# Causal attention inside a two-layer block: two score sets of the last batch in other buffers, two groups of weighted sums a set, and twenty unread products instead of twelve

## The chip, the cores and the metric

The kernel runs on one core of one Trainium2 chip. The metric is device time in microseconds (us) from one launch to its end; less is better. The engines are named as the profile names them: PE (TensorE, the matrix products), PEld (its weight loads), DVE (VectorE), ACT (ScalarE), POOL (GpSimd) and SP (SyncE, which here issues nearly all DMAs; SPq is its DMA queue).

## The reference, cut to what matters

The input x is 4 batches of 512 tokens of width 128. Two layers follow each other, each with feed-forward parts and an attention; the change touches only the softmax attention of the first layer, with 16 heads of width 8:

```python
qk = x @ w_attn.T + b_attn
q, k, v = (_heads(q), _heads(k), _heads(x))
scores = jnp.einsum('bhqd,bhkd->bhqk', q, k) * scale
scores = jnp.where(causal, scores, -jnp.inf)
y_ar = jnp.einsum('bhqk,bhkd->bhqd', jax.nn.softmax(scores, axis=-1), v)
```

A second, linear attention over the same heads uses the error `e = v[1:] - y_ar[:-1]`, so it can't start before `y_ar` of the batch is there. After the attention come a feed-forward part, eight routed experts, a recurrent linear attention and the experts once more.

## The kernel before, in words

**Sizes.** A batch has 512 tokens, cut into NT = 4 tiles of 128. The 16 heads are taken in NS = 4 sets of HL = 4 heads; one product on PE covers a tile of keys (or queries) times a tile of the other side for the four heads of a set, 512 columns. Causality leaves 10 tile pairs a set. A pair on the diagonal takes a second product, which adds the mask.

**Two passes.** The softmax needs the row maximum before the exponentials. Pass one ("maxima", `max_scores`, L1541) forms the scores with the queries as rows, pair by pair, alternately in two PSUM banks (`max_banks`, L134, one of `ps_turn`, one of `ps_accum`), and DVE reduces each (`maxima`, L1100, recorded on L1104). Maximum product m waits until reduction m-2 is done. Pass two ("scores", L1561) forms them again with the keys as rows, two pairs to a *unit*, alternately in the two halves of `ps_pair`; there the row maximum rides along as one more row of the operand, so that ACT can take the exponential of a whole unit at once (L846, recorded as `sb_work<-ps_pair`). Unit u waits until exponential u-2 is done. A batch has 20 units, five to a set (i = 0 to 4).

**Weighted sums.** `answers(b, hs, kt)` (L1576) multiplies the exponentials of key tile kt with the values. The four heads go to four groups of 32 columns of the array (shape 128*32 in the profile, where all other products here are 128*128). Key tile 0 has 512 columns, tile 1 has 384, tiles 2 and 3 have 256 and 128. After the fourth, ACT copies the set's sums out (`answers_out`, L832, recorded on L837). In ACT's order this copy stands behind the first exponential of the next set, and the second one stands behind the copy.

**Order of the work on PE** (`attention`, L1626). At step u PE issues the scores of unit u+2, one maximum product of the *next* batch, the weighted sums that are due, and a second maximum product. The sums due at step i of a set are, by L1643, key tile 0 at i = 1, tile 1 at i = 3, tiles 2 and 3 at i = 4; at i = 1 the previous set's sums are also transposed (`turn_answers`, L1588). The last batch (b = 3) has no next batch, so its steps hold no maxima. Within a batch the maxima of a set are called m0 to m9 below, two to a step: m6 and m7 at i = 3, m8 and m9 at i = 4. DVE also does work of the previous batch among the first set's maxima (a layer norm: L1001 to L1010).

**Order of the DMAs on SP** (a list written out by hand; `hold` at L310 is a wait on a semaphore). `load_exp_set` (L352) brings a set for pass two: four issues into `ring` slot 0 or 1 (L356) and one of keys into `x_sets` (L358); `max_row` (L396) then lays the row maxima into that slot. `load_max_set` (L360) does the same for pass one into `ring` slots 2 and 3 and `m_sets`. Each set has two slots that the sets take in turn, so set hs+2 can be loaded only when set hs has been read. In the loop over batches SP loads the state of the linear attention (`load_state`, L375) and the next values (`load_values`, L382), and then for each set `next_max_set(b + 1, hs)` (L388: waits for the ten maxima of that set and refills their slot) and the refill of the score slot. For the last two sets of the last batch `next_max_set` waits and loads nothing.

**Before the attention** PE runs `stay_awake(12, ...)` (L1717; L1439): products whose result nothing reads, recorded as `ps_pair<-sb_ident_bf,sb_ones_bf`. They stand ahead of batch 0's first scores, which wait for a set with its row of maxima.

Of the kernel before, what the change touches and what calls it, by code (L numbers as in the profile page):

```python
# [27 lines left out]
F32 = mybir.dt.float32  # L28
# [7 lines left out]
P = 128  # L36
D = 128
B, T = 4, 512
NT = T // P
# [64 lines left out]

MAX_PAIRS = [(qt, kt) for qt in range(NT) for kt in range(qt + 1)]
EXP_PAIRS = [(kt, qt) for kt in range(NT) for qt in range(kt, NT)]
DIAGONAL = [EXP_PAIRS.index((t, t)) for t in range(NT)]
LAST_OF_UNIT = [EXP_PAIRS[2 * i + 1][0] for i in range(NPAIR // 2)]
NM, NX, NG_X = NS * NPAIR, NS * NPAIR // 2, NPAIR // 2
STEPS = NS * NT  # L110
# [2 lines left out]
def build(nc, x_in, bias_cols, w_attn_t, w_k2_t, w_proj_t, b_proj, w1_t, w2_t, b2,  # L113
          l1_w, l1_bv, l1_wp, l1_bp, wr, mw1, mw2, consts, out):
    ctx = ExitStack()
    with ctx:
# [193 lines left out]
        def hold(eng, sem, value):  # L310


            eng.wait_ge(sem, value)
            eng.sem_inc(s["held"], 1)
# [5 lines left out]
        def _(sp):  # L320
# [61 lines left out]
            def load_values(b):  # L382
# [2 lines left out]
                    hold(sp, s["v_aug"], b)  # L385
                sp.dma_start(values_of[b % 2][:], v_scr[b].rearrange("(t p) d -> p t d", p=P)).then_inc(s["v_in"], 16)

            def next_max_set(b, hs):  # L388

                hold(sp, s["smax_mm"], NM * b + NPAIR * (hs + 1))  # L390
                if hs + 2 < NS:
                    load_max_set(b, hs + 2)
                elif b + 1 < B:
                    load_max_set(b + 1, hs + 2 - NS)

            def max_row(b, hs):  # L396

                sp.dma_start(ring[3 * HD:3 * HD + 1, hs % 2].bitcast(F32),
                             mT[HL * hs:HL * hs + HL].bitcast(F32)).then_inc(s[f"xset{hs % 2}"], 16)

            def keep_values(b):

# [53 lines left out]
            for b in range(B):  # L456
                load_state(b)
                if b + 1 < B:
                    load_values(b + 1)
                for hs in range(NS):  # L460
                    if b + 1 < B:
                        next_max_set(b + 1, hs)
                    hold(sp, s["st_mm"], NX * b + NG_X * (hs + 1))
                    if hs + 2 < NS:
                        load_exp_set(b, hs + 2)
                        max_row(b, hs + 2)
                    elif b + 1 < B:
                        load_exp_set(b + 1, hs + 2 - NS)
                if b + 1 < B:
                    hold(sp, s["max_t_evac"], b + 2)  # L470
                    for hs in range(2):
                        max_row(b + 1, hs)
            for scr in xe_scr:
                spill = scr[0:NTOK].rearrange("(p r) d -> p r d", p=P)
# [951 lines left out]
        def _(pe):  # L1426
            def mm(dst, lhsT, rhs, start=True, stop=True):
                return pe.matmul(dst, lhsT, rhs, start=start, stop=stop, skip_group_check=True)  # L1428
# [132 lines left out]
            def scores(b, u):  # L1561

                hs, i = u // NG_X, u % NG_X
                if i == 0:
                    pe.wait_ge(s[f"xset{hs % 2}"], 96 * (2 * b + hs // 2 + 1))
                if u >= 2:
                    pe.wait_ge(s["exp_done"], NX * b + u - 1)
                for a in range(2):
                    kt, qt = EXP_PAIRS[2 * i + a]
                    last = mm(pair[u % 2][:, a, :], tile(x_sets[:, hs % 2], kt), ring[:, hs % 2, :, qt * P:(qt + 1) * P],  # L1570
                              stop=kt != qt)
                    if kt == qt:
                        last = mm(pair[u % 2][:, a, :], ident_bf[:], bc(add_k_bf[:], HL), start=False)
                last.then_inc(s["st_mm"], 1)
# [51 lines left out]
            def attention(b):  # L1626
# [9 lines left out]
                for u in range(NX):  # L1636
# [3 lines left out]
                    if ahead:  # L1640
                        max_scores(b + 1, 2 * u, 2 * u + 1)
                    for kt in range(NT):
                        if (DIAGONAL[kt] + NT - kt - 1) // 2 == i:  # L1643
                            answers(b, hs, kt)
                    if hs and i == 1:
                        turn_answers(b, hs - 1)
# [67 lines left out]
            pe.wait_ge(s["ma_k"], B)  # L1714
            pe.wait_ge(s["ffn_x"], B)
            pe.wait_ge(s["ka_tok"], B)
            stay_awake(12, pair[1][:, 1])  # L1717
            pe.wait_ge(s["max_t_evac"], 1)
            for b in range(B):
                attention(b)  # L1720
# [289 lines left out]
```

## Time and profile before

| what | value |
|---|---|
| time of the kernel, median of 3 runs | 661.89 us (658.84 to 665.67) |
| span of the profiled execution | 656.1 us |
| PE, DVE, ACT, POOL busy in that span | 82%, 55%, 30%, 29% |
| mean granted clock of PE, as a share of full speed | 0.946 |
| softmax and linear attention, four batches | 114.8 to 346.5 us of the span |

The profiled execution has a span, from its first to its last instruction; its own device time isn't listed apart from that. The median of the runs is 5.8 us above the span. Times in the rows are us from the start of the span. A matrix product's recorded length includes its way through the pipeline, so products overlap: what one costs is the distance from its start to the start of the next.

### The profile page before, as it was taken

The numbers are of one execution on the slowest core, as the hardware profiler recorded it, in microseconds if no ns is written. First come the engines' busy times: TensorE is split into PE (matmuls) and PEld (weight loads), VectorE is DVE, ScalarE is ACT, GpSimd is POOL, SyncE is SP. The second block draws the span as 40 slices with busy tenths as digits, with TensorE's granted clock in tenths as the row PEclk, the third lists the DMA queues.
The fourth block names the chain that finished last, engine by engine and source line by source line (L and its number), as shares of the span: only waits on it lengthen the run. The fifth ranks groups of instructions, "written<-read, shape, count | busy, mean of one in ns | idle before, by whom it ended". The sixth has DMA issues, their size and how long they took to land.

```text
span 656.1 us, 10406 instructions
## 1 busy us (share of the span) xinstructions
PE 537.0 (82%) x3895; PEld 330.7 (50%) x3895; DVE 359.9 (55%) x942; ACT 197.1 (30%) x282; POOL 189.0 (29%) x228
## 2 busy tenths in 40 slices
PE   1878676999899898988887987994887878888893
PEld 0655332444544453454355763882455555554593
DVE  5653666466676856683063562222686978833121
ACT  1354231543144334515613630211321311110120
POOL 6575562011020102011111167462310311322153
PEclk9996789799999999999998997996998999968998
DMA  7217878732352353215199823222575274100220
GB/s 269 115 38 242 277 230 265 174 108 66 96 154 58 114 110 92 72 45 138 49 144 148 256 90 109 78 70 76 161 201 152 62 200 127 50 33 27 89 72 10
DMA packets 73666, 79.85 MB, mean 122 GB/s; under 512 B 10946, under 2 KB 50499, under 8 KB 73360
## 3 DMA queue, kind: packets, MB, share of 16 engines
q1 hardware_dynamic: 71056, 73.61, 40.9%
q0 software_dynamic: 2560, 5.58, 2.5%
q8 instruction: 31, 0.51, 0.3%
q14 instruction: 19, 0.16, 0.1%
HBM read 44.07 MB, written 35.72 MB: 122 GB/s over the span
## 4 chain that ended last, share of the span: by engine, by line
PE 51%; DVE 18%; issue 7%; DMA 7%; SPq 5%; ACT 5%; POOL 5%; POOLq 0%; DVEq 0%; ACTq 0%
PE ps_accum L1428 23%; PE ps_pair L1428 18%; PE ps_turn L1428 6%; DMA sb_ring<-sb_qs 3%; PE ps_turn L1436 3%; SPq L356 2%; DVE sb_work L1178 2%; POOL sb_rstd L569 2%; DVE sb_stats L1001 2%; DVE sb_mpart L1104 1%; SPq L350 1%; DVE sb_work L1323 1%; POOL xe_scr L589 1%; DMA sb_expert_rows<-xe_scr 1%; DVE sb_mv L1004 1%
## 5 line engine op out<-in xcount | busy, mean ns | idle before, releaser
L846 ACT ACTIVATE sb_work<-ps_pair 128x1024 f32<-128x1024 f32 x80 | 80.3, 1026 | 55.8 <-PE ps_pair L1428 54.9
L1104 DVE TENSOR_REDUCE sb_mpart<-ps_turn 128x4 f32<-128x512 f32 x80 | 55.0, 688 | 32.4 <-PE ps_turn L1428 32.3
L1428 PE MATMUL ps_pair<-sb_ring,sb_xsets 128*128 128x512 f32 x160 | 64.5, 480 | 9.7 <-DMA sb_ring<-sb_qs 5.5
L1104 DVE TENSOR_REDUCE sb_mpart<-ps_accum 128x4 f32<-128x512 f32 x80 | 55.1, 688 | 19.3 <-PE ps_accum L1428 18.6
L1428 PE MATMUL ps_pair<-sb_ident_bf,sb_ones_bf 128*128 128x512 bf16 x189 | 51.0, 426 | 12.3 <-DMA sb_x<-y_scr 8.0
L1428 PE MATMUL ps_accum<-sb_work,sb_v_aug 128*32 128x128 f32 (+3 forms) x768 | 58.2, 397 | 0.3 <-ACT sb_work L846 0.3
L1428 PE MATMUL ps_turn<-sb_ring,sb_m_sets 128*128 128x512 f32 x80 | 39.0, 487 | 9.3 <-DVE sb_mpart L1104 9.0
L1428 PE MATMUL ps_accum<-sb_ring,sb_m_sets 128*128 128x512 f32 x80 | 41.4, 518 | 4.3 <-DVE sb_mpart L1104 3.8
L567 POOL TENSOR_SCALAR sb_ve<-sb_mv 128x4 f32<-128x4 f32 x24 | 5.5, 228 | 136.3 <-DVE sb_mv L1004 131.1
L650 POOL TENSOR_TENSOR sb_e_pad<-sb_v_next,sb_y_ar 128x128 f32<-128x128 f32 x16 | 7.3, 459 | 126.5 <-DVE sb_y_ar L1148 126.5
L1428 PEld LDWEIGHTS ps_pair<-sb_ring,sb_xsets 128*128 128x128 f32 x160 | 30.7, 199 | 20.8 <-issue 7.8
L1323 DVE TENSOR_TENSOR sb_work<-ps_pair,sb_cst 128x1024 f32<-128x1024 f32 x32 | 37.5, 1215 | 1.3 <-PE ps_pair L1428 1.2
L1178 DVE TENSOR_TENSOR sb_work<-ps_pair,sb_cst 128x1024 f32<-128x1024 f32 x32 | 37.7, 1219 | 0.9
L1428 PEld LDWEIGHTS ps_pair<-sb_ident_bf,sb_ones_bf 128*128 128x128 bf16 x189 | 19.8, 108 | 36.4 <-issue 10.9
L1428 PE MATMUL ps_accum<-sb_mw,sb_work 128*128 128x128 f32 x256 | 31.3, 276 | 2.7 <-issue 2.7
L589 POOL DMA_INDIRECT xe_scr<-sb_exit_rows,sb_slot_all x16 | 15.9, 995 | 59.5 <-DVE sb_slot_all L1085 55.9
L1272 DVE SCALAR_TENSOR_TENSOR sb_y_tmp<-ps_accum,sb_expert_rows 128x128 f32<-128x128 f32 x32 | 9.8, 347 | 42.0 <-PE ps_accum L1428 42.0
L1428 PE MATMUL ps_pair<-sb_y_tmp,sb_mw 128*128 128x256 f32 x128 | 30.7, 383 | 2.0 <-ACT sb_y_tmp L902 2.0
L1428 PE MATMUL ps_pair<-sb_xs,sb_w1r 128*128 128x512 f32 x64 | 23.5, 498 | 10.1 <-DVE sb_xs L1020 6.9
L1428 PEld LDWEIGHTS ps_accum<-sb_mw,sb_work 128*128 128x128 f32 x256 | 30.0, 192 | 3.1 <-issue 3.0
L1428 PEld LDWEIGHTS ps_accum<-sb_ring,sb_m_sets 128*128 128x128 f32 x80 | 15.4, 192 | 25.6 <-DVE sb_mpart L1104 18.5
L1428 PEld LDWEIGHTS ps_accum<-sb_work,sb_v_aug 128*32 128x32 f32 x768 | 17.4, 110 | 21.3 <-issue 13.0
(251 smaller groups left out, 1013.6 us busy)
## 6 DMA issues: line engine op xcount, KB each, us to landing
sb_expert_rows<-xe_scr SPq DMA_DIRECT2D x16, 258.0 KB, 2.7
sb_m_sets<-q_scr SPq DMA_DIRECT2D x16, 256.0 KB
sb_xsets<-k_scr SPq DMA_DIRECT2D x16, 256.0 KB
sb_ka_stk<-mk_scr SPq DMA_DIRECT2D x4, 1024.0 KB
xe_scr<-sb_cst SPq DMA_DIRECT2D x4, 1024.0 KB, 13.6
sb_mw<-in_mw SPq DMA_DIRECT2D x16, 256.0 KB, 5.8
sb_ka_stk<-mk_scr SPq DMA_DIRECT2D x8, 512.0 KB
q_scr<-sb_qs SPq DMA_DIRECT2D x12, 256.0 KB, 3.4
```

Source lines behind the costliest of these rows:

```text
L356: sp.dma_start(ring[VW * hl:VW * hl + 3 * HD, i, hl].bitcast(F32), head_rows(q_scr, b, HL * hs + hl, 3 * HD)).then_inc(done, 16)
L569: pool.tensor_tensor(rstd[i][:], ve[i][:], const("minus_half"), ALU.pow).then_inc(s["rstd"], 1)
L589: pool.indirect_dma_start(xe_scr[m], bass.IndirectOffsetOnAxis(ap=slot_all[:, i:i + 1], axis=0), rows_out[m][b][:, t, :], None).then_inc(s ...
L650: pool.tensor_tensor(dst, value, answer, ALU.subtract).then_inc(s["err_pad"], 1)
L846: act.activation(banks[:, 2 * i:2 * i + 2], pair[u % 2][:], ACT.Exp, scale=SCALE).then_inc(s["exp_done"], 1)
L1001: dve.bn_stats(stats[i][:, t, :], src[:, t, :]).then_inc(s["stats"], 1)
L1104: dve.tensor_reduce(mpart[:, m // NPAIR, m % NPAIR, :], max_banks[m % 2][:].rearrange("p (h k) -> p h k", h=HL), AX.X, ALU.max).then_inc(s ...
L1178: dve.tensor_tensor(work[:, n % 4].rearrange("p a (h q) -> p (a h) q", h=HL), pair[n % 2][:].rearrange("p a (h q) -> p (a h) q", h=HL), bc ...
L1272: last = dve.scalar_tensor_tensor(out=ye[n % 2][:, g, :], in0=accum[n % 2][:, g * D:(g + 1) * D], scalar=xg[:, n % 4, g, GATE:GATE + 1], i ...
L1323: dve.tensor_tensor(work[:, n % 4].rearrange("p a (h q) -> p (a h) q", h=HL), pair[n % 2][:].rearrange("p a (h q) -> p (a h) q", h=HL), bc ...
L1428: return pe.matmul(dst, lhsT, rhs, start=start, stop=stop, skip_group_check=True)
L1436: last = pe.transpose(tile(dst, t), src[:, t, 0:D], ident)
```

## The change

It does three things.

1. Sets 2 and 3 of the last batch are loaded into the `ring` slots 2 and 3 and into `m_sets`, the buffers of the maxima, once the last maxima have read them (`load_late_set`, called by `next_max_set`). All four rows of maxima of the last batch are laid in one after another, behind `max_t_evac`. The loads that the last batch issued between its own sets are gone, and `scores` takes these two sets from the other slots.
2. The sums of key tile 1 move from step i = 3 to step i = 4, where they stand directly ahead of those of tiles 2 and 3 (`ANSWERS_BEHIND`). This holds in all four batches.
3. `stay_awake` ahead of the attention runs 20 products instead of 12.

```diff
--- before.py
+++ after.py
@@ -104,7 +104,7 @@
 
 MAX_PAIRS = [(qt, kt) for qt in range(NT) for kt in range(qt + 1)]
 EXP_PAIRS = [(kt, qt) for kt in range(NT) for qt in range(kt, NT)]
-DIAGONAL = [EXP_PAIRS.index((t, t)) for t in range(NT)]
+ANSWERS_BEHIND = [1, 4, 4, 4]
 LAST_OF_UNIT = [EXP_PAIRS[2 * i + 1][0] for i in range(NPAIR // 2)]
 NM, NX, NG_X = NS * NPAIR, NS * NPAIR // 2, NPAIR // 2
 STEPS = NS * NT
@@ -385,6 +385,14 @@
                     hold(sp, s["v_aug"], b)
                 sp.dma_start(values_of[b % 2][:], v_scr[b].rearrange("(t p) d -> p t d", p=P)).then_inc(s["v_in"], 16)
 
+            def load_late_set(hs):
+
+                i, done = hs - 2, s[f"mset{hs - 2}"]
+                for hl in range(HL):
+                    sp.dma_start(ring[VW * hl:VW * hl + 3 * HD, hs, hl].bitcast(F32),
+                                 head_rows(q_scr, B - 1, HL * hs + hl, 3 * HD)).then_inc(done, 16)
+                sp.dma_start(m_sets[:, i].bitcast(F32), set_rows(k_scr, B - 1, hs)).then_inc(done, 16)
+
             def next_max_set(b, hs):
 
                 hold(sp, s["smax_mm"], NM * b + NPAIR * (hs + 1))
@@ -392,11 +400,14 @@
                     load_max_set(b, hs + 2)
                 elif b + 1 < B:
                     load_max_set(b + 1, hs + 2 - NS)
+                else:
+                    load_late_set(hs)
 
             def max_row(b, hs):
 
-                sp.dma_start(ring[3 * HD:3 * HD + 1, hs % 2].bitcast(F32),
-                             mT[HL * hs:HL * hs + HL].bitcast(F32)).then_inc(s[f"xset{hs % 2}"], 16)
+                late = b == B - 1 and hs >= 2
+                sp.dma_start(ring[3 * HD:3 * HD + 1, hs if late else hs % 2].bitcast(F32),
+                             mT[HL * hs:HL * hs + HL].bitcast(F32)).then_inc(s[f"mset{hs - 2}" if late else f"xset{hs % 2}"], 16)
 
             def keep_values(b):
 
@@ -461,14 +472,16 @@
                     if b + 1 < B:
                         next_max_set(b + 1, hs)
                     hold(sp, s["st_mm"], NX * b + NG_X * (hs + 1))
+                    if b == B - 1:
+                        continue
                     if hs + 2 < NS:
                         load_exp_set(b, hs + 2)
                         max_row(b, hs + 2)
-                    elif b + 1 < B:
+                    else:
                         load_exp_set(b + 1, hs + 2 - NS)
                 if b + 1 < B:
                     hold(sp, s["max_t_evac"], b + 2)
-                    for hs in range(2):
+                    for hs in range(NS if b + 2 == B else 2):
                         max_row(b + 1, hs)
             for scr in xe_scr:
                 spill = scr[0:NTOK].rearrange("(p r) d -> p r d", p=P)
@@ -1561,13 +1574,17 @@
             def scores(b, u):
 
                 hs, i = u // NG_X, u % NG_X
-                if i == 0:
+                late = b == B - 1 and hs >= 2
+                slot, keys = (hs, m_sets[:, hs - 2]) if late else (hs % 2, x_sets[:, hs % 2])
+                if i == 0 and late:
+                    pe.wait_ge(s[f"mset{hs - 2}"], 80 * 2 * B + 96)
+                elif i == 0:
                     pe.wait_ge(s[f"xset{hs % 2}"], 96 * (2 * b + hs // 2 + 1))
                 if u >= 2:
                     pe.wait_ge(s["exp_done"], NX * b + u - 1)
                 for a in range(2):
                     kt, qt = EXP_PAIRS[2 * i + a]
-                    last = mm(pair[u % 2][:, a, :], tile(x_sets[:, hs % 2], kt), ring[:, hs % 2, :, qt * P:(qt + 1) * P],
+                    last = mm(pair[u % 2][:, a, :], tile(keys, kt), ring[:, slot, :, qt * P:(qt + 1) * P],
                               stop=kt != qt)
                     if kt == qt:
                         last = mm(pair[u % 2][:, a, :], ident_bf[:], bc(add_k_bf[:], HL), start=False)
@@ -1640,7 +1657,7 @@
                     if ahead:
                         max_scores(b + 1, 2 * u, 2 * u + 1)
                     for kt in range(NT):
-                        if (DIAGONAL[kt] + NT - kt - 1) // 2 == i:
+                        if ANSWERS_BEHIND[kt] == i:
                             answers(b, hs, kt)
                     if hs and i == 1:
                         turn_answers(b, hs - 1)
@@ -1714,7 +1731,7 @@
             pe.wait_ge(s["ma_k"], B)
             pe.wait_ge(s["ffn_x"], B)
             pe.wait_ge(s["ka_tok"], B)
-            stay_awake(12, pair[1][:, 1])
+            stay_awake(20, pair[1][:, 1])
             pe.wait_ge(s["max_t_evac"], 1)
             for b in range(B):
                 attention(b)
```

## Rows read from the trace of the kernel before

**Rows 1.** The page's chain that ended last, share of the span by engine.

```profile
PE 51%; DVE 18%; issue 7%; DMA 7%; SPq 5%; ACT 5%; POOL 5%; POOLq 0%; DVEq 0%; ACTq 0%
```

**Rows 2.** Timeline, all engines, around the start of the attention.

```profile
109.72 2.75 PE L1428 MATMUL ps_pair<-sb_ident_bf,sb_ones_bf 128*128 128x512 bf16 x12
...
111.75 1.37 SPq L398 DMA_DIRECT2D sb_ring<-sb_qs  x2
...
114.80 0.76 PE L1428 MATMUL ps_pair<-sb_ring,sb_xsets 128*128 128x512 f32 x1 [2.32 <-DMA sb_ring<-sb_qs]
...
122.16 1.06 PE L1428 MATMUL ps_accum<-sb_work,sb_v_aug 128*32 128x512 f32 x8
```

**Rows 3.** Windows there: PE, PEld, DVE, ACT, POOL busy, then PEclk, DMA, GB/s.

```profile
114.00:115.00 1.00, 0.20 (x1) 0.23 (x1) 0.00 (x0) 0.00 (x0) 0.00 (x0) 0.80 0.31 105
...
121.00:122.00 1.00, 1.00 (x5) 0.35 (x3) 0.58 (x1) 0.19 (x1) 0.00 (x0) 0.78 1.06 131
```

**Rows 4.** Timelines of PE and of ACT, first unit of the last batch.

```profile
299.17 0.48 PE L1428 MATMUL ps_pair<-sb_ring,sb_xsets 128*128 128x512 f32 x1
...
300.14 1.02 ACT L846 ACTIVATE sb_work<-ps_pair 128x1024 f32<-128x1024 f32 x1
```

**Rows 5.** Timeline of PE, an idle stretch in the last batch, and the window.

```profile
335.68 0.46 PE L1428 MATMUL ps_turn<-sb_v_next,sb_ka_tok 128*128 128x128 f32 x2 [1.74 <-POOL sb_v_next L651]
...
335.00:337.00 2.00, 1.00 (x4) 0.59 (x4) 2.00 (x3) 0.00 (x0) 0.58 (x2) 1.00 1.23 203
```

**Rows 6.** Timeline, second batch, set 1, steps 3 and 4.

```profile
209.77 0.85 PE L1428 MATMUL ps_accum<-sb_work,sb_v_aug 128*32 128x384 f32 x8
...
209.88 0.69 DVE L1104 TENSOR_REDUCE sb_mpart<-ps_turn 128x4 f32<-128x512 f32 x1 [0.80 <-PE ps_turn L1428]
...
210.55 0.50 PE L1428 MATMUL ps_accum<-sb_ring,sb_m_sets 128*128 128x512 f32 x1
...
210.89 0.62 PE L1428 MATMUL ps_pair<-sb_ring,sb_xsets 128*128 128x512 f32 x2
...
211.35 0.39 PE L1428 MATMUL ps_turn<-sb_ring,sb_m_sets 128*128 128x512 f32 x1
...
211.67 0.86 PE L1428 MATMUL ps_accum<-sb_work,sb_v_aug 128*32 128x256 f32 x16
```

**Rows 7.** Timeline, second batch, set 3, steps 3 and 4.

```profile
219.44 0.50 PE L1428 MATMUL ps_turn<-sb_ring,sb_m_sets 128*128 128x512 f32 x1
...
219.61 0.69 DVE L1104 TENSOR_REDUCE sb_mpart<-ps_accum 128x4 f32<-128x512 f32 x1 [0.22 <-PE ps_accum L1428]
...
220.99 0.46 PE L1428 MATMUL ps_turn<-sb_ring,sb_m_sets 128*128 128x512 f32 x1
```

**Rows 8.** Timeline, second batch, set 0, steps 3 and 4.

```profile
187.19 1.11 DVE L1010 TENSOR_SCALAR sb_qf<-sb_x,sb_mv,sb_rstd 128x128 f32<-128x128 f32 x4 [0.41 <-POOL sb_rstd L569]
...
188.22 0.69 DVE L1104 TENSOR_REDUCE sb_mpart<-ps_turn 128x4 f32<-128x512 f32 x1
...
188.96 0.49 PE L1428 MATMUL ps_turn<-sb_ring,sb_m_sets 128*128 128x512 f32 x1 [0.55 <-DVE sb_mpart L1104]
```

**Rows 9.** Timelines of PE and of ACT, last batch, sets 0 and 1.

```profile
306.50 1.94 ACT L846 ACTIVATE sb_work<-ps_pair 128x1024 f32<-128x1024 f32 x2 [0.85 <-PE ps_pair L1428]
...
307.08 0.85 PE L1428 MATMUL ps_accum<-sb_work,sb_v_aug 128*32 128x384 f32 x8
...
307.86 0.73 PE L1428 MATMUL ps_pair<-sb_ring,sb_xsets 128*128 128x512 f32 x2
...
309.45 0.59 ACT L837 COPY sb_y_tmp<-ps_accum 128x512 f32<-128x512 f32 x1 [1.01 <-PE ps_accum L1428]
...
314.55 0.50 PE L1428 MATMUL ps_pair<-sb_ring,sb_xsets 128*128 128x512 f32 x1 [0.30 <-DMA sb_ring<-sb_qs]
```

**Rows 10.** Timeline of SP, its DMA issues near the last batch.

```profile
285.73 1.51 SPq L356 DMA_DIRECT2D sb_ring<-q_scr  x4
...
288.25 1.21 SPq L398 DMA_DIRECT2D sb_ring<-sb_qs  x2
```

## Prediction

> **What bounds the kernel now.** I read the chain that ended last first: PE carries half of it, DVE 18%, DMA and SP's queue 12% together [rows 1]. PE's order is fixed, so each part of the change is worth what it takes out of PE's sequence between two of its waits. Then I read the timeline at the places that the diff touches, and the windows for the granted clock. The reader is to see four things.
>
> At the start of the attention PE has run its 12 unread products and then sits idle for 2.32 us, until the row of maxima has landed [rows 2]. The granted clock falls to half in that gap (0.80 over the microsecond from 114, so from about 114.6) and comes back within the microsecond from 121 (0.78, so at about 121.44) [rows 3]. These are the levels 1.2 and 2.4 GHz. The first score product takes 0.76 us there, against 0.48 in the last batch [rows 2, 4].
>
> In a batch with maxima, PE and DVE go hand in hand: a maximum product can't start before the reduction two before it has ended. In the last batch there are no maxima, and PE goes hand in hand with ACT instead.
>
> The wait for the late load in the last batch is short: 0.30 us of idle PE ahead of set 2's first product [rows 9].
>
> **Part 3, eight more unread products.** Twelve took 2.75 us, at most 0.23 each [rows 2]; eight more take 1.8 us and end at about 114.3, still 0.5 us ahead of the first score product at 114.80. So they cover the gap and delay nothing; if the row landed 1.8 us earlier they would cost up to 1.8. The idle time that is left is 0.5 us. Does the clock hold over that? In the last batch PE idled 1.74 us, and the window around it is granted 1.00 [rows 5]. I take it that it holds.
>
> What that is worth: I lay the sequence of the slow stretch out again with distances at full clock. A product of 512 columns costs 0.23 (two stand between 210.89 and 211.35) [rows 6]. From the first product to the first exponential it is 0.97 in the last batch [rows 4]: the exponential starts at 115.77 and ends, 1.02 later, at 116.79. The third unit waits for it and ends its three products at about 117.8. Then come m0 (two products), m1 (one), a unit (three) and m2 (two), 8 x 0.23 = 1.84, and 0.1 for the wait of m2 for its reduction: the first weighted sums start at about 119.7 instead of 122.16 [rows 2], **-2.5 us**. All that follows waits for PE's progress, so I pass it on whole. Bounds: 0 if the clock falls all the same; -3.4 if all of the 6.8 us at half clock were PE's own time.
>
> **Part 2, the sums of key tile 1 beside those of tiles 2 and 3.** What a group of sums costs beyond its columns: the 384 columns of tile 1 take 0.78 from their start to the next product, the 256 + 128 of tiles 2 and 3 the same kind of group; the 512 of tile 0 last 0.21 longer than the 384 [rows 2, 6], so 128 columns are 0.21, 384 are 0.63, and 0.15 is fixed. The product ahead of a group takes 0.32 instead of 0.23 (211.35 to 211.67), the one behind 0.34 (210.55 to 210.89) [rows 6]. So a separate group costs 0.15 + 0.09 + 0.11 = 0.35, and a merged one saves that, if PE has nothing to wait for in the place where the group stood.
>
> It has. In three places the old group stood beside a wait that it hid:
>
> *Batches 0 to 2, sets 1 and 2, and set 0 of batch 0 (seven sets).* m6 is done just before its reduction starts at 209.88, which ends at 210.57. m8 needs that. Without tile 1's group, m7 and two products of scores are through 4 x 0.23 after m6, at 210.77 as an end; but m8 can only start at 210.61 and end, 0.50 later, at 211.11. The merged group starts at 211.03 and takes 0.78 + 0.63 = 1.41, to 212.44. Before, the group of tiles 2 and 3 began at 211.67 and was through at 212.45 [rows 6]. Saving 0.0: the 0.35 goes into a new wait for DVE. The waits for the loads of sets 2 and 3 lie ahead of this stretch and are hung on the end of the maxima, so they move with it and change nothing.
>
> *Batches 0 to 2, set 3 (three sets).* No scores stand between here. m6 starts at 219.44, m7 must wait for the reduction that runs from 219.61 to 220.30, m8 for the next one, which ends at most 0.69 later, at 220.99. m8 started at 220.99 before too [rows 7]: tile 1's group cost nothing where it was. Behind m8 it adds its columns, **+0.63** each, 1.9 together. The last maxima, their reduction and the linear attention all stand behind it.
>
> *Set 0 of batches 1 and 2 (two sets).* DVE runs the layer norm's last step from 187.19 to 188.30 and only then the reduction that m8 waits for; m8 starts at 188.96 after 0.55 of idle PE [rows 8]. Again the group was free and now isn't: +0.63 each, 1.3 together.
>
> *Last batch.* At i = 4 the scores of unit 6 wait for exponential 4, which ends at 307.52. Tile 1's group filled the time from 307.08 [rows 9]. Now PE idles until 307.56, the unit's two products end at 308.29, the merged group at 309.70, and ACT's copy goes from 309.45 to 309.76: +0.31, and the exponentials behind the copy with it. Sets 1 and 2 the same by pattern; in set 3 nothing stands between the two places. **+0.9** together.
>
> Part 2 sums to +1.9 + 1.3 + 0.9 = **+4.1**. Bounds: -5.3 (15 sets x 0.35) and +10 (16 x 0.63).
>
> The Trainium skill, in TensorEngine Tiling (Array Packing), section Key Properties, says that a change of the tiling mode drains the engine. By that rule alone one pair of switches less per set is a gain in each set, and the whole part would be -5.3. The 0.35 above agrees with it; that nothing else steps in is what the rows speak against.
>
> **Part 1, the early loads.** The loads ahead of set 2 are gone, and the 0.30 us of idle PE with them: the product that ended at 314.55 + 0.50 ends 0.23 after its predecessor's end at 314.25, at 314.48 [rows 9]. That is **-0.6**; set 3 shows no such wait.
>
> What it adds lies in batch 2, where SP gets two late sets of five issues (1.51 for four, some 1.9 a set) and four rows instead of two (0.6 each) [rows 10]. The first late set stands a whole set earlier and has that much more cover. The second stands at 285.73, moves the last score set to 287.6 and the rows from 288.25 to 289.5, and the last row is issued at 291.9. At the start of the attention a row was used 3.1 us after its issue (111.75 to 114.80) [rows 2], so all lie by 295.0; the first scores of the last batch run at 299.17 [rows 4]. There are 4.2 us of cover, and each microsecond beyond that would cost one. Behind them SP waits for the end of batch 2 anyway. Cost 0, at most 1.
>
> **The sum.** -2.5 + 4.1 - 0.6 = **+1.0 us** on the profiled execution, 656.1 to 657.1 of span. I add the same to the median, as what lies around the span isn't touched: 661.9 + 1.0 = **662.9 us**, no change that can be told: a measurement of this kernel tells about 1%, or 6.6 us.
>
> **Rivals.**
>
> *The clock gives nothing (ends slower).* Either the clock falls in the shorter gap too, or in most executions it doesn't fall there even before, since the fall hangs on one gap of 2.3 us, and 1.74 us did not bring it [rows 2, 5]. The runs of before spread over 6.8 us, so executions do differ in something of this size. Then only parts 1 and 2 are left: +3.5, 665.4. It decides from the point where part 3 gives less than 3.5; the forecast itself is past it by 1.0. For it: one trace only. Against it: in that trace the fall is plain, and the gap shrinks to a quarter.
>
> *The saved switches are kept (ends faster).* If the new waits on DVE and ACT are shorter than I lay them out, say since the reductions start earlier, the 0.35 stays in 15 sets: -5.3 - 0.6 - 2.5 = -8.4, 653.5. For it: the drain is real in every group. Against it: the waits of m7 and m8 are read from two rows each.
>
> *The late loads don't do what they say.* The rows land too late for the last batch, or the load that was 0.30 late was nearly hidden, so that the scores just wait for ACT instead. The latter takes the -0.6 away, 663.5; the former needs more than 4.2 us and costs what lies beyond, 1 to 3 us, 664 to 666.
>
> **How the numbers follow.** The forecast 0.60, the clock rival 0.22, the kept switches 0.10, the loads 0.05, anything else 0.03. The forecast's own range is 660.5 to 665.0 (0 to -3.4 for the clock shifts it most). For 8 in 10 I go up to 668.0, past the clock rival with another 2.6 for the spread between executions, and down to 656.5, which leaves out most of the kept switches. Faster by over 1% (below 655.3): most of the kept switches, 0.08. Slower by over 1% (above 668.5): the clock rival with a further gap that newly brings the clock down, 0.05. Within 1%: 0.87.
>
> **What would show it.** Part 3: 20 unread products that end before the row lands, a granted clock of 1.00 through the microseconds 115 to 121, the first sums 2.5 us sooner after the first score product than 7.36. Part 2: two groups a set, and a new idle time of 0.3 us "<- DVE sb_mpart" ahead of m8, in set 3 one of 0.4 ahead of m7; the time from set 3's m6 to the end of its m9 longer by 0.6; in the last batch an idle time before unit 6's scores that ACT ends. Part 1: no DMA wait in the last batch. Wrong would be a half clock at the start all the same, sets of batches 0 to 2 that are shorter by 0.3 each, or a wait for a DMA ahead of the last batch's first scores.

## Result, and the profile after

The changed kernel takes 664.2 us in the median of 20 runs, against 660.25 us for the kernel before beside them (20 runs). The ratio is 1.0075, interval 1.0047 to 1.0103: slower by 5.0 us (0.0075 x 660.25), between 3.1 and 6.8. All times here are medians of all runs, while the ratios are of the fast runs, those within 1.5% of their kernel's fastest, and so leave out four of the 20 here and four of the 12 of experiment 9. The slowdown is inside the predicted range and within 1%, but 4.0 us above the +1.0 that the steps gave. A second series of the same kernel gave 1.0099 (1.0065 to 1.0133).

The profiled execution has a span of 665.6 us against 656.1, further apart than the runs as a whole. Its chain of waits hardly shows a change: PE 50%, DVE 19%, DMA 6%, ACT 6%, each within a point of before [rows 1].

So the reading goes by places. ACT's copy of each set's sums is the mark: the time from one copy to the next is the time of a set. A batch ends with another copy of ACT, behind its linear attention. From the first score product of the attention to the copy that ends the last batch is 231.74 us before (114.80 to 346.54) and 238.51 after (115.16 to 353.67), +6.77:

| stretch | before | after | difference |
|---|---|---|---|
| first score to first copy | 14.06 | 13.24 | -0.82 |
| set 3 of batches 0, 1, 2 (third to fourth copy) | 9.72, 9.71, 9.69 | 10.36, 10.35, 10.37 | +1.96 |
| set 0 of batches 1, 2 (from the end of the batch ahead) | 14.74, 14.72 | 16.84, 16.60 | +3.98 |
| last batch, sets 0 to 3 | 10.00, 8.37, 7.79, 6.84 | 10.34, 8.15, 8.16, 6.85 | +0.50 |
| linear attention of the last batch | 14.09 | 15.50 | +1.41 |
| all else | | | -0.26 |

The remaining 2.8 us of the span's +9.5 lie ahead of and behind the attention, where the change touches nothing but the unread products. One execution differs from another by that much: the part behind the attention, the same in all kernels here, takes 309.5 us before, 311.9 after, and up to 315.6 (experiment 1).

**Set 2 of the second batch**, timeline, after. It answers to [rows 6], where it is called set 1; the copy that ends it, at 212.59 there, is the batch's third. A line gives the start, the length and what ran; in brackets stand the engine's idle time just before it and what ended that:

```profile
211.35 0.50 PE L1441 MATMUL ps_pair<-sb_ring,sb_xsets 128*128 128x512 f32 x1 [0.35 <-DMA sb_ring<-sb_qs]
...
212.58 0.69 DVE L1117 TENSOR_REDUCE sb_mpart<-ps_turn 128x4 f32<-128x512 f32 x1 [0.84 <-PE ps_turn L1441]
...
213.32 0.50 PE L1441 MATMUL ps_turn<-sb_ring,sb_m_sets 128*128 128x512 f32 x1
...
213.76 1.50 PE L1441 MATMUL ps_accum<-sb_work,sb_v_aug 128*32 128x384 f32 x24
...
215.33 0.59 ACT L850 COPY sb_y_tmp<-ps_accum 128x512 f32<-128x512 f32 x1 [1.95 <-PE ps_accum L1441]
```

and its two ends before:

```profile
208.66 0.50 PE L1428 MATMUL ps_pair<-sb_ring,sb_xsets 128*128 128x512 f32 x1 [0.31 <-DMA sb_ring<-sb_qs]
...
212.59 0.59 ACT L837 COPY sb_y_tmp<-ps_accum 128x512 f32<-128x512 f32 x1 [1.92 <-PE ps_accum L1428]
```

The merged group (24 products, 1.50 us) starts 0.44 behind m8, and m8 starts 0.74 after the reduction that it waits for began. From the first score of step 3 to ACT's copy it is 3.98 us (the copy starts at 215.33); before it was 3.93 (208.66 to 212.59). A group of weighted sums less, and nothing gained. The idle time of 0.3 us ahead of m8 that was forecast isn't listed as one, but m8 starts 0.05 after the end of its reduction.

**Set 3 of the second batch**, after, answers to [rows 7]:

```profile
222.16 0.50 PE L1441 MATMUL ps_turn<-sb_ring,sb_m_sets 128*128 128x512 f32 x1
...
222.33 0.69 DVE L1117 TENSOR_REDUCE sb_mpart<-ps_accum 128x4 f32<-128x512 f32 x1 [0.22 <-PE ps_accum L1441]
...
223.08 0.50 PE L1441 MATMUL ps_accum<-sb_ring,sb_m_sets 128*128 128x512 f32 x1 [0.41 <-DVE sb_mpart L1117]
...
223.68 0.50 PE L1441 MATMUL ps_turn<-sb_ring,sb_m_sets 128*128 128x512 f32 x1
...
224.11 1.50 PE L1441 MATMUL ps_accum<-sb_work,sb_v_aug 128*32 128x384 f32 x24
```

Where tile 1's group stood, PE now idles 0.41 us ahead of m7 until DVE is through; m8 starts 1.52 after m6, as before (1.55). The group's columns are added behind m8.

**Set 0 of the second batch**, after, answers to [rows 8], and the window over its group of sums (columns: window, share of it, PE, PEld, DVE, ACT, POOL busy, granted clock of PE, DMA, GB/s):

```profile
187.24 1.12 DVE L1023 TENSOR_SCALAR sb_qf<-sb_x,sb_mv,sb_rstd 128x128 f32<-128x128 f32 x4 [0.41 <-POOL sb_rstd L582]
188.27 0.69 DVE L1117 TENSOR_REDUCE sb_mpart<-ps_turn 128x4 f32<-128x512 f32 x1
...
189.01 0.67 PE L1441 MATMUL ps_turn<-sb_ring,sb_m_sets 128*128 128x512 f32 x1 [1.15 <-DVE sb_mpart L1117]
189.62 2.79 PE L1441 MATMUL ps_accum<-sb_work,sb_v_aug 128*32 128x384 f32 x24
...
190.00:191.00 1.00, 1.00 (x12) 0.30 (x8) 0.42 (x1) 0.00 (x0) 0.00 (x0) 0.50 0.00 0
...
192.00:193.00 1.00, 1.00 (x11) 0.49 (x3) 0.00 (x0) 0.53 (x2) 0.00 (x0) 0.71 0.00 0
```

The idle time ahead of m8 was 0.55 and is now 1.15, since the group that stood there is gone. What no step had: from about 189.2 on the granted clock is 0.50, so the same 24 products take 2.79 us instead of 1.50. The clock is back within the microsecond from 192. Batch 2 repeats this (2.77 us).

**Start of the attention**, PE's timeline and windows, after; it answers to [rows 2, 3]:

```profile
109.25 4.48 PE L1441 MATMUL ps_pair<-sb_ident_bf,sb_ones_bf 128*128 128x512 bf16 x20
115.16 0.47 PE L1441 MATMUL ps_pair<-sb_ring,sb_xsets 128*128 128x512 f32 x1 [1.43 <-DMA sb_ring<-sb_qs]
...
121.68 1.07 PE L1441 MATMUL ps_accum<-sb_work,sb_v_aug 128*32 128x512 f32 x8
...
116.00:117.00 1.00, 0.54 (x3) 0.11 (x1) 0.00 (x0) 0.80 (x1) 0.00 (x0) 1.00 0.73 123
...
118.00:119.00 1.00, 1.00 (x4) 0.52 (x2) 0.00 (x0) 0.20 (x2) 0.00 (x0) 0.50 0.81 168
```

Twenty products leave 1.43 us of idle PE, not 0.5, and the clock falls all the same, only later (half from 117.5 to 120.9). From the first score to the first sums it is 6.52 us, against 7.36 before and the 4.9 that was forecast.

**Last batch.** PE waits for ACT 0.43 us ahead of the scores of unit 6. The DMA wait of 0.30 ahead of set 2 [rows 9] is gone:

```profile
312.78 0.73 PE L1441 MATMUL ps_pair<-sb_ring,sb_xsets 128*128 128x512 f32 x2 [0.43 <-ACT sb_work L859]
313.44 1.50 PE L1441 MATMUL ps_accum<-sb_work,sb_v_aug 128*32 128x384 f32 x24
```

### The profile page after: what moved, and what is told of

The parts are those of the page before. It is cut to its first block, busy times and chain, and to the rows that moved or that the text cites. A ratio compares the mean times of both kernels' runs of the same rounds, so it can differ in the third digit from the quotient of the medians.

```text
span 665.6 us, 10422 instructions
## 1 busy us (share of the span) xinstructions
PE 539.3 (81%) x3903; PEld 334.3 (50%) x3903; DVE 359.3 (54%) x942; ACT 197.1 (30%) x282; POOL 189.0 (28%) x228
## 4 chain that ended last, share of the span: by engine, by line
PE 50%; DVE 19%; issue 7%; DMA 6%; ACT 6%; POOL 5%; SPq 5%; POOLq 0%; DVEq 0%; ACTq 0%
PE ps_accum L1441 23%; PE ps_pair L1441 17%; PE ps_turn L1441 6%; DMA sb_ring<-sb_qs 3%; DVE sb_mpart L1117 3%; PE ps_turn L1449 2%; POOL sb_rstd L582 2%; DVE sb_work L1191 2%; DVE sb_stats L1014 2%; SPq L356 2%; ACT sb_work L859 1%; SPq L350 1%; DVE sb_work L1336 1%; DMA sb_cols<-in_bias_cols 1%; POOL xe_scr L602 1%
## 5 line engine op out<-in xcount | busy, mean ns | idle before, releaser
L1441 PE MATMUL ps_pair<-sb_ring,sb_xsets 128*128 128x512 f32 x140 | 55.1, 470 | 7.0 <-DMA sb_ring<-sb_qs 3.4
L1441 PEld LDWEIGHTS ps_pair<-sb_ring,sb_xsets 128*128 128x128 f32 x140 | 26.8, 196 | 14.9 <-issue 6.0
L1441 PEld LDWEIGHTS ps_accum<-sb_work,sb_v_aug 128*32 128x32 f32 x768 | 19.5, 113 | 22.9 <-issue 15.6
L1441 PEld LDWEIGHTS ps_turn<-sb_ring,sb_m_sets 128*128 128x128 f32 x80 | 15.4, 192 | 25.1 <-DVE sb_mpart L1117 22.7
```

## Experiments

**1. The merged sums alone**, on the kernel before:

```diff
-DIAGONAL = [EXP_PAIRS.index((t, t)) for t in range(NT)]
+ANSWERS_BEHIND = [1, 4, 4, 4]
...
-                        if (DIAGONAL[kt] + NT - kt - 1) // 2 == i:
+                        if ANSWERS_BEHIND[kt] == i:
```

> Part 2 alone (key tile 1's weighted sums at step 4), on the kernel before. Theory A (the moved group leaves a place where it hid a wait for DVE or ACT, and stands bare behind that wait, where the longer idle of PE can bring the clock to half as well): slower by 4 to 7 us, ratio 1.006 to 1.011; the distance from the third to the fourth copy of the sums in batches 0 to 2 grows from 9.7 to 10.35 us; set 0 of batches 1 and 2 grows by 0.6 (clock stays) to 2.1 us (clock falls). Theory B (the loss comes from the early loads or from the products): ratio 1.000 within 0.002. Theory C (one switch of the tiling mode less is kept): ratio 0.992.

Measured: 667.2 us (6 runs), ratio 1.0122 (1.0070 to 1.0175). By the copies: set 3 takes 10.36 in all three batches (+0.64, +0.65, +0.67), set 0 of batches 1 and 2 takes 15.36 and 15.37 (+0.62, +0.65), and the last batch's four sets sum to 33.51 against 33.00 (+0.51). Together 3.7 us. The ratio says 8.0 us (4.6 to 11.5), more than the copies show. The mean granted clock of these six runs is 0.938, against 0.947 in the runs of before beside them; why it is lower isn't known. The start of the attention, and set 0 of the second batch:

```profile
113.78 0.47 PE L1428 MATMUL ps_pair<-sb_ring,sb_xsets 128*128 128x512 f32 x1 [1.78 <-DMA sb_ring<-sb_qs]
...
187.19 0.50 PE L1428 MATMUL ps_turn<-sb_ring,sb_m_sets 128*128 128x512 f32 x1 [1.16 <-DVE sb_mpart L1104]
187.63 1.50 PE L1428 MATMUL ps_accum<-sb_work,sb_v_aug 128*32 128x384 f32 x24
```

Ahead of m8 stands the same idle time as in the changed kernel (1.16), and here the clock holds: the group takes 1.50. So 0.63 is the cost of the order itself, and the further 1.2 to 1.5 of the changed kernel's trace is the clock, which falls in one execution and not in another. This kernel's start has the clock held too, with 12 unread products and an idle time of 1.78 us; the first sums come 5.06 behind the first score. One execution was thus 2.3 us quicker there than the profile of before, with nothing done for it.

**2. The early loads alone**: the changed kernel with `ANSWERS_BEHIND = [1, 3, 4, 4]`, which is the old order, and 12 unread products:

```diff
-ANSWERS_BEHIND = [1, 4, 4, 4]
+ANSWERS_BEHIND = [1, 3, 4, 4]
...
-            stay_awake(20, pair[1][:, 1])
+            stay_awake(12, pair[1][:, 1])
```

> Part 1 alone (sets 2 and 3 of the last batch loaded early). Theory A: the 0.30 us of idle PE for the load in the last batch is gone and nothing else, -0.6 us, ratio 0.999, not to be told from 1; set 1 of the last batch 7.8 instead of 8.4 us between its copies. Theory B: the first rows of the last batch land late, PE waits ahead of the last batch's first scores, ratio 1.003 or more.

Measured: 660.24 us (12 runs), ratio 1.0033 (0.9997 to 1.0069), not told from 1. By the copies the last batch's sets take 10.02, 7.80, 7.81, 6.85: set 1 is 0.57 shorter (8.37 before), the batch 0.52, and no idle time stands ahead of set 2's first product (the last line below). Nor is a wait listed ahead of the batch's first scores.

```profile
111.38 4.59 PE L1441 MATMUL ps_pair<-sb_ident_bf,sb_ones_bf 128*128 128x512 bf16 x12
115.62 0.58 PE L1441 MATMUL ps_pair<-sb_ring,sb_xsets 128*128 128x512 f32 x1
...
312.51 0.58 PE L1441 MATMUL ps_pair<-sb_ring,sb_m_sets 128*128 128x512 f32 x1
```

The load was worth what it was said to be worth. In the changed kernel, where the merged sums stand ahead of it, it is worth nothing: set 1 takes 8.15 there and 8.15 with the merged sums alone. At the start of this execution the 12 unread products ran at half clock (4.59 us instead of 2.75) and reached to the first score; behind them the clock was full, and the first sums came 5.17 after the first score.

**3. Twenty unread products alone:**

```diff
-            stay_awake(12, pair[1][:, 1])
+            stay_awake(20, pair[1][:, 1])
```

> Part 3 alone (20 unread products). Theory A (they only shorten the idle time ahead of the first scores): between -2.5 us (the clock stays at full) and 0 (it falls all the same, or did not fall in most executions before), ratio 0.996 to 1.000; from the first score product to the first weighted sums 4.9 to 7.4 us. Theory B (they delay the first scores): slower by up to 1.8 us, ratio 1.003, and no idle time of PE between the last unread product and the first score.

Measured: 661.01 us (12 runs), ratio 1.0013 (0.9979 to 1.0047): between 1.4 us won and 3.1 lost, so the forecast 2.5 is ruled out for the runs as a whole. In its profile the row lands 7.05 us after the first unread product, the idle time is 2.57 and the clock falls to half:

```profile
107.40 4.48 PE L1428 MATMUL ps_pair<-sb_ident_bf,sb_ones_bf 128*128 128x512 bf16 x20
114.45 0.47 PE L1428 MATMUL ps_pair<-sb_ring,sb_xsets 128*128 128x512 f32 x1 [2.57 <-DMA sb_ring<-sb_qs]
...
121.73 1.56 PE L1428 MATMUL ps_accum<-sb_work,sb_v_aug 128*32 128x512 f32 x8
...
116.00:120.00 4.00, 3.33 (x8) 2.01 (x8) 0.77 (x2) 2.46 (x3) 0.00 (x0) 0.50 0.98 164
```

**4. Early loads and 26 unread products, old order of the sums:** experiment 2's kernel with

```diff
-            stay_awake(12, pair[1][:, 1])
+            stay_awake(26, pair[1][:, 1])
```

> Parts 1 and 3 without part 2, and 26 unread products instead of 20, so that they reach to the landing of the row. Theory A: the clock stays at full behind them, -0.6 and -2.5 us, 3 us faster than before, ratio 0.995; the granted clock is 1.00 from the first score to the first weighted sums, which lie 4.9 us apart instead of 7.36. If the clock fell in few executions of before, ratio 0.998. Theory B (the products or the loads cost): ratio 1.002 or more.

Measured: 659.79 us (12 runs), ratio 1.0033 (0.9995 to 1.0070). In the profile the 26 products reach to the landing, no idle time is left and the clock is 1.00 throughout:

```profile
109.39 5.78 PE L1441 MATMUL ps_pair<-sb_ident_bf,sb_ones_bf 128*128 128x512 bf16 x26
114.81 0.58 PE L1441 MATMUL ps_pair<-sb_ring,sb_xsets 128*128 128x512 f32 x1
...
119.99 1.07 PE L1441 MATMUL ps_accum<-sb_work,sb_v_aug 128*32 128x512 f32 x8
...
115.00:118.00 3.00, 2.18 (x10) 1.17 (x8) 0.00 (x0) 1.94 (x2) 0.00 (x0) 1.00 0.69 199
118.00:122.00 4.00, 4.00 (x22) 1.81 (x20) 2.45 (x4) 2.05 (x2) 0.00 (x0) 1.00 0.99 176
```

The first sums come 5.18 after the first score, 2.2 sooner than before: the size of the forecast is right where the clock holds. Yet the runs show no gain, where 3 us were forecast, and the span (656.2) is that of before. In this execution the linear attention of the last batch ran partly at half clock, 15.48 us instead of 14.09, which takes back 1.4. The attention as a whole is still 2.5 us shorter (229.20 against 231.74), and the part behind it, which the edit doesn't touch, 2.6 longer (312.13 against 309.53).

**5 and 6. Shorter reductions, without and with the merged sums** (one execution each). Both take only 32 of each 128 keys into the maxima, so that a reduction takes 0.29 us instead of 0.69 and PE hardly waits for one outside set 0:

```diff
-max_banks[m % 2][:].rearrange("p (h k) -> p h k", h=HL),
+max_banks[m % 2][:].rearrange("p (h k) -> p h k", h=HL)[:, :, 0:P // 4],
```

> The kernel before, with the maxima's reductions over 32 of the 128 keys of a tile (so the row maxima are not the true ones). DVE is then done far sooner. Theory A: PE no longer waits for reductions; the third to the fourth copy in batches 0 to 2, 9.7 us before, shrinks by the waits for DVE that were in it, to 9.2 to 9.5 us. It is the base for the next run.

> The same short reductions (row maxima not the true ones) together with part 2. Theory A (the switch of the tiling mode is saved, but a wait for DVE takes its place): with DVE out of the way the saving shows, the distance from the third to the fourth copy in batches 0 to 2 is 0.3 us SHORTER than in the run with short reductions and without part 2, where with whole reductions part 2 made it 0.64 us LONGER; the distances of the other sets are shorter by 0.3 too or the same. Theory C (a merged group is dearer by itself, in whatever place): it is longer by about 0.6 us here too.

Measured: 652.75 us and, with the merged sums, 654.91. One run of each tells nothing of the whole time, so only places are compared. Set 2 of the second batch, without them:

```profile
203.31 0.50 PE L1428 MATMUL ps_pair<-sb_ring,sb_xsets 128*128 128x512 f32 x1 [1.16 <-DMA sb_ring<-sb_qs]
...
206.34 0.86 PE L1428 MATMUL ps_accum<-sb_work,sb_v_aug 128*32 128x256 f32 x16
...
207.27 0.59 ACT L837 COPY sb_y_tmp<-ps_accum 128x512 f32<-128x512 f32 x1 [1.94 <-PE ps_accum L1428]
```

and with them:

```profile
202.25 0.50 PE L1428 MATMUL ps_pair<-sb_ring,sb_xsets 128*128 128x512 f32 x1 [0.64 <-DMA sb_ring<-sb_qs]
...
203.47 0.29 DVE L1104 TENSOR_REDUCE sb_mpart<-ps_turn 128x4 f32<-128x128 f32 x1 [1.53 <-PE ps_turn L1428]
...
204.30 1.50 PE L1428 MATMUL ps_accum<-sb_work,sb_v_aug 128*32 128x384 f32 x24
...
205.87 0.59 ACT L837 COPY sb_y_tmp<-ps_accum 128x512 f32<-128x512 f32 x1 [1.59 <-PE ps_accum L1428]
```

From the first score to the copy: 3.96 us without (203.31 to 207.27), 3.62 with (202.25 to 205.87). **0.34** saved, where at full reductions the same edit saved nothing (3.93 to 3.97 in experiment 1). In all seven sets of this kind it saves 0.31 to 0.35. So a separate group has its price, 0.35 by the prediction, and it was DVE's reduction that ate it.

Two kinds of set were a miss. Set 3 takes 9.12 to 9.13 with, 9.05 to 9.07 without (which is less than the 9.2 expected). It doesn't gain even then, as no scores stand between its maxima: m7 still waits for product and reduction of m5, one behind the other. Set 0 of batches 1 and 2 takes 14.37 both times with, 13.74 and 13.72 without, 0.63 and 0.65 more as with full reductions, since the layer norm on DVE still stands ahead of m8's reduction:

```profile
182.30 0.50 PE L1428 MATMUL ps_turn<-sb_ring,sb_m_sets 128*128 128x512 f32 x1 [1.54 <-DVE sb_mpart L1104]
182.73 1.50 PE L1428 MATMUL ps_accum<-sb_work,sb_v_aug 128*32 128x384 f32 x24
```

The idle time of 1.54 us ahead of m8 is longer than in the changed kernel, and the clock held in both batches.

**7. A filler in set 0:** the changed kernel with four unread products ahead of m8 in batches 1 and 2.

```diff
+                    if ahead and b and u == 4:
+                        stay_awake(4, turn[0])
                     if ahead:
                         max_scores(b + 1, 2 * u, 2 * u + 1)
```

> The changed kernel with 4 more unread products ahead of maximum m8 in set 0 of batches 1 and 2, where PE idles for 1.15 us. Theory A (the idle time there is what brings the clock down): the granted clock is 1.00 through the merged group, set 0's first copy comes 15.4 us after the copy that ends the batch before, where the changed kernel has 16.84 and 16.60; 2 to 3 us faster than the changed kernel where that falls in both batches, ratio to before 1.002 to 1.007. Rival (the clock falls by chance, or it is the group's own length): 16.6 or more again in at least one of the two batches, with a granted clock of 0.50 in it.

Measured: set 0 of batches 1 and 2 takes 15.37 both times, as in experiment 1 and against 16.84 and 16.60:

```profile
188.51 1.04 PE L1441 MATMUL ps_turn<-sb_ident_bf,sb_ones_bf 128*128 128x512 bf16 x4
189.83 0.50 PE L1441 MATMUL ps_turn<-sb_ring,sb_m_sets 128*128 128x512 f32 x1 [0.29 <-DVE sb_mpart L1117]
190.26 1.50 PE L1441 MATMUL ps_accum<-sb_work,sb_v_aug 128*32 128x384 f32 x24
...
190.00:191.00 1.00, 1.00 (x13) 0.37 (x17) 1.00 (x2) 0.00 (x0) 0.52 (x1) 1.00 0.00 0
```

With 0.29 of idle PE in the place of 1.15 the clock is 1.00. But it held without a filler too, in experiments 1 and 6, so this one trace doesn't show that the filler did it. The time is 664.26 us (12 runs), ratio 1.0064 (1.0024 to 1.0105), which isn't told apart from the changed kernel's: the gain of 2 to 3 us on it isn't shown.

**8. The changed kernel again**, for a second trace:

> The changed kernel once more, beside the filler run. Theory A: ratio 1.005 to 1.010; set 0 of batches 1 and 2 takes 16.6 to 16.9 us where the clock falls in it and 15.4 where it holds; third to fourth copy 10.35 in batches 0 to 2 in either case.

Measured: 665.45 us (12 runs), ratio 1.0099 (1.0065 to 1.0133). Set 3 takes 10.36, 10.35, 10.35 and set 0 takes 16.94 and 16.44, again at half clock behind m8:

```profile
192.00:193.00 1.00, 1.00 (x16) 0.32 (x10) 0.00 (x0) 0.00 (x0) 0.00 (x0) 0.50 0.00 0
```

At the start this execution went a third way: the unread products themselves ran at half clock (6.33 us for 20), no idle time was left, the clock then held, and the first sums came 5.19 behind the first score. Here the scores waited for the products: the first score came 5.06 us after the issue of its row, and 2.6 to 4.4 in the traces with an idle time, so at least 0.6 us was lost (an estimate from these).

**9. The merged sums ahead of m8** (on the kernel before; set 3 and the last batch keep the old order). If the loss comes from where the group stands, the other side of the waiting product is the place for it: there it covers the reduction, and the switch is saved as well.

```diff
+                    merged = ahead and hs < NS - 1
-                    if ahead:
+                    if ahead and not (merged and i == 4):
                         max_scores(b + 1, 2 * u, 2 * u + 1)
                     for kt in range(NT):
-                        if (DIAGONAL[kt] + NT - kt - 1) // 2 == i:
+                        if (1, 4 if merged else 3, 4, 4)[kt] == i:
                             answers(b, hs, kt)
                     if hs and i == 1:
                         turn_answers(b, hs - 1)
+                    if merged and i == 4:
+                        max_scores(b + 1, 2 * u, 2 * u + 1)
```

> On the kernel before: in sets 0 to 2 of the batches with maxima the sums of key tiles 1, 2 and 3 stand together at step 4, but ahead of maximum m8 instead of between m8 and m9; set 3 and the last batch as before. Theory A (the merged group saves its switch where it covers the wait of m8 for its reduction): from the first score product of step 3 to the copy 3.0 to 3.4 us in sets 1 and 2 against 3.93 before (the sums no longer have m8 ahead of them), the whole set 0.35 us shorter; set 0 of batches 1 and 2 shorter by 0.9; third to fourth copy 9.7 plus 0.3 at most (the fourth has m8 ahead again). Sum 7 x 0.35 + 2 x 0.9 = 4.3 us faster, ratio 0.9935. Rival (the merged group itself is what costs, as in the change): ratio 1.003 or more.

Measured: 656.66 us (12 runs) against 658.7, ratio 0.9929 (0.9886 to 0.9971): faster than both kernels, against before by 4.7 us by the ratio (1.9 to 7.5) but by 2.0 by the medians. By the copies, batches 0 to 2 behind their first copies, without the linear attentions, take 123.0 us in this trace and in that of experiment 10, against 127.1 before: 4.1 less. Set 2 of the second batch:

```profile
202.16 0.50 PE L1428 MATMUL ps_pair<-sb_ring,sb_xsets 128*128 128x512 f32 x1
...
203.39 0.69 DVE L1104 TENSOR_REDUCE sb_mpart<-ps_turn 128x4 f32<-128x512 f32 x1 [0.64 <-PE ps_turn L1428]
...
203.97 1.50 PE L1428 MATMUL ps_accum<-sb_work,sb_v_aug 128*32 128x384 f32 x24
...
205.40 0.50 PE L1428 MATMUL ps_turn<-sb_ring,sb_m_sets 128*128 128x512 f32 x1
...
205.54 0.59 ACT L837 COPY sb_y_tmp<-ps_accum 128x512 f32<-128x512 f32 x1 [1.35 <-PE ps_accum L1428]
```

The group starts while the reduction runs (until 204.08), and m8 goes behind it with no idle time. First score to copy: 3.38 us, against 3.93 before; part of that is only that m8 stands behind the copy now. To the next step's first score it is 3.85 against 4.18, 0.33 less, about the price of a group. Set 0 of batches 1 and 2 takes 13.70 and 13.72, 1.0 less than before, and set 3, which keeps the old order, 0.2 more (9.94 to 9.96).

**10. The same with early loads and 26 unread products** (experiments 4 and 9 together):

> The same order of the sums, with the early loads and 26 unread products: all three parts, the second in the place that covers the wait. Theory A: 4.3 us from the sums, 0.6 from the loads, 0 to 2.5 from the products: 5 to 7 us faster than before, ratio 0.989 to 0.993. Rival (loads or products cost, as the ratio of 1.003 of the run without the sums would allow): ratio 0.995 or more, that is, no better than the sums alone.

Measured: 654.74 us (12 runs), ratio 0.9951 (0.9916 to 0.9986). Faster than both kernels too, and not told apart from experiment 9: what the loads and the products add to it doesn't show in the runs. The 5 to 7 us of the expectation aren't reached (4.0 by the medians); that is its rival.

## Why the prediction was right in its range, and which step failed

*How near it came.* The time, 662.9, is only 1.3 below the measured 664.2 by luck: it starts from 661.89, the median of three runs, and 20 runs give 660.25. The range was met since it left room for the rival "The clock gives nothing", chance 0.22, which came about in place of the forecast; the half clock behind m8 came on top of it in the profile.

*Part 2: the mechanism holds, and the sizes but for the last batch.* Set 3: +0.63 forecast, +0.64 to +0.67 measured. Set 0 of batches 1 and 2: +0.63, and +0.62 and +0.65 where the clock holds (experiment 1). Seven sets at 0.0: sets 1 and 2 of batches 0 to 2 sum to -0.29 over all in the changed kernel's trace, and [rows 6] against the rows after give +0.05. Two of the three idle times came where they were told, 0.41 ahead of m7 in set 3 and, in the last batch, 0.43 that ACT ends. The last batch lost 0.51, not 0.9: sets 0 and 2 lose 0.36 and 0.38, but set 1 gains 0.22. The rival of the kept switches falls: a separate group costs its 0.35 (experiments 5 and 6), but the place had a wait under it. The Trainium skill, in TensorEngine Tiling (Array Packing), section Key Properties, says that a change of the tiling mode drains TensorE. The 0.31 to 0.35 saved fit that, though no run here tells the drain from other costs of a group. What decided was DVE.

*Part 1 and part 2 together.* The loads alone gave -0.52 (-0.6 forecast), the merged sums alone +0.51 in the last batch (+0.9 forecast), both +0.50 (+0.3 forecast). They don't add: with the merged sums alone no wait for the load is listed ahead of set 2 any more, and PE waits for ACT one unit later in the same step (0.29 us, and 0.43 in the changed kernel). The rows of SP's queue brought no new wait, as said.

*Part 3 is the step that failed:* "The idle time that is left is 0.5 us. [...] I take it that it holds." The 0.5 came from one execution, in which the row landed 5.08 us after the first unread product. In the three traces with 20 products that ran at full clock it landed 5.91 (changed kernel), 7.05 (experiment 3) and 6.52 us (experiment 7) after it; the idle time was 1.43, 2.57 and 2.04 us, and the clock fell in all three. That is the half clock at the start which the prediction named as its sign of being wrong. Nor was the fall the rule before: of the four traces with 12 products and full reductions only that of before had it. In experiments 1, 2 and 9 the first sums came 5.05 to 5.17 us after the first score with nothing done for it, so in most executions there may have been nothing to win. Part 3 gave -0.84 in the changed kernel's trace (7.36 to 6.52) and between -1.4 and +3.1 in the runs of experiment 3. The size was right where the clock held (2.2 to 2.3 us). With part 3 at nothing, the prediction's own sum is +3.5, inside the measured 3.1 to 6.8: that is its rival "the clock gives nothing".

*A term was missing.* That the clock can fall at the longer idle time ahead of m8 was priced nowhere but in the tail of the range. It cost 1.47 and 1.23 more (16.84 and 16.60 against 15.37) in batches 1 and 2 of one trace and 1.57 and 1.07 in the other. It didn't fall with 0.55 us of idle time there (eight sets in experiments 2 to 4 and before), nor with the filler, but neither in experiments 1 and 6 with 1.16 and 1.54: that the longer idle time brings it down is likely, not shown.

*What stays open.* How much of the +5.0 is this term. The directly measured cost of the order, 3.7, is within the interval by itself. Each run has its mean granted clock: 0.9445 over 32 runs of the changed kernel, 0.9455 over 75 of before, so on the whole the clock is hardly lower. Over all runs 0.01 less of it goes with about 3.5 us more; by that line the second series of the changed kernel is 5.5 us above before at an equal clock, and the kernel with the filler 5.0 (estimates, good to about 1.6 each). So a lower clock isn't the main part, and the runs with the filler don't show its share. The half clock in the last batch's linear attention (15.50 us against 14.09) appears in both traces of the changed kernel, but also in experiments 4, 6, 7 and 10, with and without merged sums behind m8, and not in experiment 1; what brings it about wasn't tried. Experiments 2, 3 and 4 lie 0.1 to 0.3% above before where less was forecast. Each is not told from 1, and experiment 10 beside 9 shows no such cost, but that the loads or the products cost something in a place not read isn't ruled out.

## What to carry to other kernels

A group of work that stands in front of a waiting instruction may be free where it is; before moving it, ask what the engine does in the gap that it leaves, and price the move at the full length of the group. If it is to be merged, put the merged group ahead of the instruction that waits, not behind it: by the copies the same merge cost 3.7 us behind m8, with set 3 and the last batch included, and won 4.1 ahead of it without them. A gain that hangs on the clock in one recorded gap should be taken as a chance, not as a term: look at several executions, and see whether the mean clock of the runs moves.

## What the runs showed of the hardware that was not expected

The length of an idle stretch alone didn't tell whether the granted clock falls behind it. After 1.15 us ahead of m8 it was half in both traces of the changed kernel, and after 1.16 in the same place it held in experiment 1, after 1.54 in experiment 6. At the start it fell after 1.43 us (changed kernel) and held after 1.78 (experiment 1) and 2.00:

```profile
112.25 0.48 PE L1428 MATMUL ps_pair<-sb_ring,sb_xsets 128*128 128x512 f32 x1 [2.00 <-DMA sb_ring<-sb_qs]
```

That is experiment 9, with 12 unread products ahead; its first sums come 5.05 us later. And a full clock at the start didn't show in the runs: with 26 products it was 1.00 there, while the mean clock over the 12 runs of experiment 4, 0.9452, is that of before (0.9455). In most traces with 12 products, too, the clock held there.
